# Flamingo block: attention shares split into bf16 parts before they are transposed, and transposed by DMAs

## The reference

```python
x = x + jnp.tanh(g_xattn[0]) * _L0_xattn_ref(_layernorm(x, axis=-1), ctx_512, ...)
x = x + jnp.tanh(g_ffn[0]) * _L0_ffn_ref(_layernorm(x, axis=-1), ...)

# inside _L0_xattn_ref, 16 heads, 128 context rows of 128 channels
q_big = jnp.einsum('bshk,hkq->bshq', q_hk, w_kc_q)
q_r = jnp.einsum('bshq,hqr->bhsr', q_big, W_qr)
k_r = jnp.einsum('bld,hdr->bhlr', kv_rope, W_kr)
scores = jnp.einsum('bhsr,bhlr->bhsl', q_r, k_r)
attn = jax.nn.softmax(scores, axis=-1)
ctx_c = jnp.einsum('bhsl,bld->bhsd', attn, kv_rope)
ctx_lat = jnp.einsum('bhsd,hkd->bshk', ctx_c, w_kc_kv)
out = ctx_lat.reshape(b, s, H * K) @ Wo.T
```

## Time and profile before

| | |
|---|---|
| median of 3 runs | 2187.03 us (2184.39 to 2189.79) |
| span of the profiled execution, first to last instruction | 2184.7 us |
| mean granted TensorE clock over the span | 0.980 |
| PE busy | 2083.8 us, 95% |
| DVE, ACT, POOL busy | 1064.1, 761.5, 621.5 us (49%, 35%, 28%) |
| attention, PE's first to last `o` matmul | 96.2 to about 906 us |
| one step of the attention, mean of a round | 6.48 us |

### The profile page before, as it was taken

The page is one execution under the profiler, slowest core; times in us unless marked ns, Lnnn a source line. Parts: engine busy times, 40 slices in busy tenths (PEclk is TensorE's granted clock), DMA queues, the critical chain, the costliest instruction groups (busy, mean ns, idle before and its releaser), DMA issues.

```text
span 2184.7 us, 35089 instructions
## 1 busy us (share of the span) xinstructions
PE 2083.8 (95%) x13060; PEld 1300.5 (60%) x13060; DVE 1064.1 (49%) x2190; ACT 761.5 (35%) x2089; POOL 621.5 (28%) x680
## 2 busy tenths in 40 slices
PE   7799999999999999895599999999999999999999
PEld 7566666666666666441147777777775444444444
DVE  5776777666666666460134333333332433332333
ACT  4555555555655665320012333333321000000000
POOL 5523333333333452107322223332311220100101
PEclk9999999999999999997699999999999999999999
DMA  8212211111111321321114333333322330211202
GB/s 273 60 38 71 69 61 55 55 55 55 56 62 59 107 78 44 119 70 20 59 40 148 119 113 120 122 116 120 122 89 79 106 140 25 73 50 65 77 15 82
DMA packets 88237, 179.66 MB, mean 82 GB/s; under 512 B 13120, under 2 KB 19008, under 8 KB 88128
## 3 DMA queue, kind: packets, MB, share of 16 engines
q1 hardware_dynamic: 74560, 140.33, 18.9%
q0 software_dynamic: 13568, 37.79, 5.9%
HBM read 121.39 MB, written 56.70 MB: 82 GB/s over the span
## 4 chain that ended last, share of the span: by engine, by line
PE 83%; issue 6%; DVE 6%; ACT 3%; POOL 1%; DMA 1%; DVEq 0%; SPq 0%; ACTq 0%; POOLq 0%
PE score L777 14%; PE o L541 12%; PE score L694 10%; PE o L791 7%; PE p_bank L595 5%; PE m_bank L694 5%; PE p_bank L694 5%; PE o L707 5%; PE c_bank L554 3%; PE score L572 3%; DVE arena L1002 3%; PE c_bank L707 3%; PE t_bank L707 3%; PE t_bank L562 2%; PE p_bank L599 1%
## 5 line engine op out<-in xcount | busy, mean ns | idle before, releaser
L541 PE MATMUL o<-arena 128*128 128x512 bf16 x1536 | 355.0, 380 | 10.6 <-DVE arena L1002 10.6
L777 PE MATMUL score<-arena 128*128 128x256 bf16 (+1 forms) x2880 | 335.1, 272 | 3.2 <-issue 1.7
L777 PEld LDWEIGHTS score<-arena 128*128 128x128 bf16 (+1 forms) x2880 | 292.7, 106 | 44.2 <-issue 2.7
L1362 POOL TENSOR_TENSOR arena<-arena 128x512 f32<-128x512 f32 x128 | 133.2, 1041 | 426.5 <-DVE arena L1018 424.6
L541 PEld LDWEIGHTS o<-arena 128*128 128x128 bf16 x1536 | 148.6, 99 | 171.3 <-DVE arena L1002 16.4
L694 PE MATMUL score<-arena 128*128 128x512 bf16 x1056 | 240.0, 381 | 1.0 <-ACT arena L951 0.7
L829 ACT ACTIVATE arena<-score,arena 128x128 f32<-128x128 f32 x512 | 181.1, 367 | 159.0 <-DVE arena L1042 157.8
L1306 DVE TENSOR_TENSOR arena<-arena,score 128x256 f32<-128x256 f32 (+1 forms) x120 | 50.6, 422 | 307.7 <-ACT arena L971 307.7
L1002 DVE TENSOR_TENSOR arena<-p_bank,arena 64x512 bf16<-64x512 f32 (+1 forms) x184 | 126.9, 690 | 139.9 <-ACT arena L880 119.7
L595 PE MATMUL p_bank<-arena 128*128 128x256 bf16 x1536 | 179.8, 273 | 1.8 <-DVE arena L1002 1.8
L694 PEld LDWEIGHTS score<-arena 128*128 128x128 bf16 x1056 | 102.2, 97 | 132.6 <-issue 5.9
(11 more groups left out here) (157 smaller groups left out, 3126.2 us busy)
## 6 DMA issues: line engine op xcount, KB each, us to landing
xrow_d<-arena SPq DMA_DIRECT2D x80, 256.0 KB, 2.0
arena<-w_expert SPq DMA_DIRECT2D x32, 544.0 KB
...
arena<-x SPq DMA_DIRECT2D x32, 256.0 KB, 4.6
x_d<-arena SPq DMA_DIRECT2D x32, 256.0 KB, 2.0
xn_d<-arena SPq DMA_DIRECT2D x32, 256.0 KB, 4.5
xT_d<-arena SPq DMA_DIRECT2D x32, 256.0 KB, 2.2
```

What stands on the lines that cost most here:

```text
L541: mm = pe.matmul(o_bank[b % 2][:, :], lhsT=cT[:, a, h, :], rhs=M_w[:, w, 4 * hg + h, :], start=(hg == 0 and n == 0), stop=(hg == 3 and n = ...
L777: mm = pe.matmul(gu_bank[n1 % 2][0:IW[j], c * 256:(c + 1) * 256], lhsT=wx[e % 2][:, a, col:col + IW[j]], rhs=xgT[q % 2][:, w, t, :], start ...
L1362: pool.tensor_tensor(prob[:, u % 4], prob[:, u % 4], rden[:, u % 4, :].unsqueeze(2).broadcast_to([P, 4, S]), ALU.mult).then_inc(normed, 1)
```

## The change

The normalised shares are no longer kept as float32 and transposed by PE. POOL's multiplication now writes the high part directly as bf16 in row layout (`share[..., HI]`), and DVE makes the low part from `prob`, `rden` and the high part with four `scalar_tensor_tensor` instructions of 128x128, one for each head (`share_lo`). SP then issues one transposing DMA for each unit, from `share` (128 partitions x 1024 bf16: two parts, four heads) to `pT` (eight 128x128 squares), and PE waits for its landing (`pt_in`) before `c_bank`. PE's transposes, ACT's copy of `pT` high and DVE's `pT` low are gone. `prob` has two buffers in place of four, `share` and `pT` two each; POOL's multiplication of u waits for the landing of unit u-2, ACT's exponentials of u for `share_lo` of u-2. To make room, `zero_ids` now lies on `logits` and ACT waits once for its DMA, and the routing tables move onto a weight ring. Allocations are rounded to 8 words. Inside the loop SP adds a semaphore increment (`turn_begun`) between its wait and the DMA.

The places in the steps: POOL's instruction stays where it was. DVE's four stand where `pT` low stood, between `cT` low and the row maximum, but they are on unit k+3 instead of k+2. SP's DMA stands first in each step.

```diff
@@ -81,11 +81,9 @@
         route_sb = words(2 * P + E)
         token_sb = words(NB).bitcast(I32)
         one, waited = words(1), words(16)
-        zero_ids = words(E * CAP // P).bitcast(I32)
-        logits = words(NB * E).rearrange("p (b e) -> p b e", e=E)
-        slot_of = words(2 * NB).bitcast(I32).rearrange("p (b c) -> p b c", c=2)
-        scatter_to = words(2 * NB).bitcast(I32).rearrange("p (b c) -> p b c", c=2)
-        weight_of = words(2 * NB).rearrange("p (b c) -> p b c", c=2)
+        logits_region = words(NB * E)
+        logits = logits_region.rearrange("p (b e) -> p b e", e=E)
+        zero_ids = logits_region[:, 0:E * CAP // P].bitcast(I32)
 
 
         bm_at = taken[0]
@@ -116,11 +114,13 @@
         rope_a = words(256)
         rope_b = words(256)
 
-        prob_region = words(4 * 512)
-        prob = prob_region.rearrange("p (u h n) -> p u h n", u=4, h=4)
+        prob_region = words(2 * 512)
+        prob = prob_region.rearrange("p (u h n) -> p u h n", u=2, h=4)
+        share = [halves(words(512)).rearrange("p (l h n) -> p l h n", l=2, h=4) for _ in range(2)]
+        pT = [halves(words(512)).rearrange("p (l n) -> p l n", l=2)]
         kr_at = taken[0]
         pT_region = words(512)
-        pT = halves(pT_region).rearrange("p (l n) -> p l n", l=2)
+        pT.append(halves(pT_region).rearrange("p (l n) -> p l n", l=2))
         cT_region = words(512)
         cT = halves(cT_region).rearrange("p (l h n) -> p l h n", l=2, h=4)
         neg_max = words(16).rearrange("p (u h) -> p u h", u=4)
@@ -343,6 +345,13 @@
         def _(sp):
             def step(k, it):
                 m = k % 8
+                u = k + 3
+                if within(u, NU):
+                    wait(sp, share_lo, u + 1, 16, it)
+                    if it is not None:
+                        sp.sem_inc(turn_begun, 1)
+                    sp.dma_start_transpose(pT[u % 2].rearrange("p l (h n) -> p (l h) n", h=4),
+                                           share[u % 2].rearrange("p l h n -> p (l h n)")).then_inc(pt_in[u % 2], 16)
                 if m == 1:
                     g = (k + 23) // 8
                     if within(g, NG):
@@ -546,21 +555,14 @@
                 u = k + 1
                 if within(u, NU):
                     g, b = u // 8, u // 4
-                    wait(pe, pt_lo, u + 1, 16, it)
+                    wait(pe, pt_in[u % 2], 16 * (u // 2 + 1), 128, it)
                     wait(pe, ct_lo, u, 16, it)
                     if u % 8 == 0:
                         wait(pe, ropeN_step, 6 * (g + 1), 12, it)
                     for n, (a, w) in enumerate(PASSES):
-                        mm = pe.matmul(c_bank[:, :], lhsT=kvN[g % 2][:, a, b % 2, :], rhs=pT[:, w, :],
+                        mm = pe.matmul(c_bank[:, :], lhsT=kvN[g % 2][:, a, b % 2, :], rhs=pT[u % 2][:, w, :],
                                        start=(n == 0), stop=(n == 2))
                     mm.then_inc(ct_mm, 1)
-                u = k + 2
-                if within(u, NU):
-                    wait(pe, normed, u + 1, 16, it)
-                    wait(pe, pt_lo, u, 16, it)
-                    for h in range(4):
-                        mm = pe.transpose(t_bank[:, h * S:(h + 1) * S], prob[:, u % 4, h, :], ident_sb)
-                    mm.then_inc(pt_mm, 1)
                 u = k + 4
                 if within(u, NU):
                     g, b, hg = u // 8, u // 4, u % 4
@@ -816,17 +818,14 @@
                 if within(u, NU):
                     wait(act, ct_mm, u + 1, 16, it)
                     act.copy(cT[:, HI].rearrange("p h n -> p (h n)"), c_bank[:, :]).then_inc(ct_hi, 1)
-                u = k + 2
-                if within(u, NU):
-                    wait(act, pt_mm, u + 1, 16, it)
-                    act.copy(pT[:, HI, :], t_bank[:, :]).then_inc(pt_hi, 1)
                 if k % 2 == 1:
                     upper_piece(k + 12, it)
                 u = k + 4
                 if within(u, NU):
                     wait(act, maxed, u + 1, 16, it)
+                    wait(act, share_lo, u - 1, 16, it)
                     for h in range(4):
-                        mm = act.activation(prob[:, u % 4, h, :], score_bank[u % 2][:, h * S:(h + 1) * S], ACT.Exp,
+                        mm = act.activation(prob[:, u % 2, h, :], score_bank[u % 2][:, h * S:(h + 1) * S], ACT.Exp,
                                             bias=neg_max[:, u % 4, h:h + 1], accum_out=den[:, u % 4, h:h + 1])
                     mm.then_inc(exped, 1)
                 if k % 2 == 0:
@@ -937,6 +936,7 @@
                 wait(act, gu_mm, v + 1, 22, it)
                 act.activation(silu[v % 2], gate_bank[v % 2][:, :], ACT.Silu).then_inc(silu_done, 1)
 
+            act.wait_ge(ids_zero, 16)
             run_steps(act, step, NU + 3)
             silu_step(0, None)
             for k in range(NU + 4, LAST_STEP + 1):
@@ -1031,10 +1031,14 @@
                     lower(cT[:, LO].rearrange("p h n -> p (h n)"), c_bank[:, :],
                           cT[:, HI].rearrange("p h n -> p (h n)")).then_inc(ct_lo, 1)
                 links(*((3, 4) if m == 0 else (12, 13)))
-                u = k + 2
+                u = k + 3
                 if within(u, NU):
-                    wait(dve, pt_hi, u + 1, 16, it)
-                    lower(pT[:, LO, :], t_bank[:, :], pT[:, HI, :]).then_inc(pt_lo, 1)
+                    wait(dve, share_hi, u + 1, 16, it)
+                    for h in range(4):
+                        i = dve.scalar_tensor_tensor(out=share[u % 2][:, LO, h, :], in0=prob[:, u % 2, h, :],
+                                                     scalar=rden[:, u % 4, h:h + 1], in1=share[u % 2][:, HI, h, :],
+                                                     op0=ALU.mult, op1=ALU.subtract)
+                    i.then_inc(share_lo, 1)
                 links(*((5,) if m == 0 else (14,)))
                 u = k + 4
                 if within(u, NU):
@@ -1359,9 +1363,10 @@
                 u = k + 3
                 if within(u, NU):
                     wait(pool, inverted, u + 1, 16, it)
-                    pool.tensor_tensor(prob[:, u % 4], prob[:, u % 4],
+                    wait(pool, pt_in[u % 2], 16 * (u // 2), 128, it)
+                    pool.tensor_tensor(share[u % 2][:, HI], prob[:, u % 2],
                                        rden[:, u % 4, :].unsqueeze(2).broadcast_to([P, 4, S]),
-                                       ALU.mult).then_inc(normed, 1)
+                                       ALU.mult).then_inc(share_hi, 1)
                 if m in (4, 5):
                     b = 2 * (c - 1) + m - 4
                     if within(b, NB):
```

12 lines of the change are left out of this document (7 added, 5 removed).

## The result

The changed kernel takes **2368.85 us** (median, 2366.97 to 2371.8) against 2187.47 for the kernel before (2184.39 to 2189.79): a ratio of 1.0833, 95% interval 1.0817 to 1.0848. It is slower by 181 us, where 153 was forecast, and inside the range.

The account below looks back on a forecast made before the run. PE was taken to bound the attention. Waits of 2.3 + 4.9 + 4.1 + 2.0 less 3.5 gave +9.8 us a round, +153 us over 16 rounds after a deduction for the first: 2340 us, range 2235 to 2450.

Parts of the forecast that it names:

- transposes gone: Four PE transposes fewer in each of 128 units: 56 us of PE time, 3.5 us a round gained.
- place 1: Steps 0 and 1: DVE's low shares held up by POOL; PE waits 2.7 before `o` of m = 2, 2.3 more.
- place 2: Load of `x` for m = 3, issued behind the transposing DMA: PE waits 4.9 us before `o` of m = 4.
- place 3: In m = 5 DVE's low shares wait for POOL's multiplication behind its rotary chain: PE waits 4.1 us in m = 6.
- the rest: Smaller waits of the same kind in steps 4 and 7: between 0 and 4, taken as 2.0 us a round.
- What bounds the kernel: The attention is PE bound; an edit that takes work from PE can gain only that, 3.5 us a round.
- The price of the new DVE work: Four new 128x128 DVE instructions: 0.30 each, 0.96 for four against 0.68; 1.4 later in m = 0 beside POOL.
- The clock case: Rival: PE's clock falls to the 1.2 GHz level in the new waits, giving 2404 us; chance 0.15.
- 16 x 4 = 64 more: Low-clock stretches of 2 us at places 2 and 3, in 16 rounds: 64 us on top of the forecast.
- The covers hold better: Rival: only half of the 13.3 of waits appears, +3.1 a round, about 2245 us; chance 0.18.
- The slow transfer: Rival: the transposing DMA takes longer than a step allows, deciding from near 6.5 us; 2640 us or more, chance 0.10.
- Faster: Rival: new waits swallowed if `x` lands in time and POOL's chain ends 4 earlier; 2138 us, chance 0.08.

Follow-up runs that it names:

- dummy matmuls: Changed kernel with 34 unused 512-column matmuls a round added on PE in front of the waits in m = 2, 4 and 6: 2359.07 us.
- PE's part: Kernel before, with three of the four PE transposes of a unit left out from unit 8 on: 2173.65 us, ratio 0.9953.
- the version with all moves: Changed kernel, loads of x first in m = 2, row maximum before low shares, POOL's second rotary chain spread, its first after low shares: 2152.77 us.

## Why the prediction was right, and where it was off

Per round, its terms beside the round of the changed kernel and the round with the dummy matmuls (idle time and dummies together):

| term | forecast | changed kernel | with dummies |
|---|---|---|---|
| transposes gone | -3.5 | -3.5 | -3.5 |
| place 1, less the 0.4 of before | 2.3 | 2.1 | 1.5 |
| place 2 | 4.9 | 4.06 | 4.83 |
| place 3 | 4.1 | 3.26 | 4.23 |
| the rest | 2.0 | none seen | 0.34 + 0.46 + 0.96 = 1.8 |
| PE's work at the low clock | 0 | 54.22 - 47.91 = 6.3 | 4.37 - 2.76 = 1.6 (one group of `o`) |
| sum | 9.8 | 12.2 | 10.4 |
| round, measured, less 51.81 | | 12.20 | 10.83 |

(47.91 is PE's 51.41 of work before, less 3.5. The 6.3 is of the round shown, 5.7 in the mean of the ten; some 0.3 of it are gaps too short to be marked, as PE goes on from the scores in 0.82 and not in 0.65 where it then waits. The 0.4 missing in the last column is mostly of that kind too.)

- **What bounds the kernel, right.** PE's starts were the sums of its own work, so the edit could gain at most 3.5 a round, and the new waits counted in full. (That the 3.5 could all be gained was too high: with DVE as close as it was, under half of PE's part came through when it was taken alone.) The earlier trace rows held the warning: in 500 us only 1.4 of POOL's idle time before its multiplication ended with its own chain, at no cost, and the same order became 4.45 of DVE's time in one round.
- **The price of the new DVE work, close.** 0.346 for one (median) against 0.30, 1.14 for four against 0.96, and 2.08 in m = 0, where the forecast had 412.4 - 410.37 = 2.0. The interpolation between 4 and 512 columns was a little low, and the bound from above, 0.37, was nearer.
- **Place 1, right in size (2.48 against 2.7) and in cause**, shown by the wait in front of POOL's chain.
- **Place 2, right.** Issue 1.23 against 1.0, landing of `x` 6.7 after it against 6.52, wait 4.06 against 4.9; with the clock held up it is 4.83. Shown by the loads put first.
- **Place 3, right as a place**, 3.26 against 4.1 and 4.23 with the clock held up. But its price is not the price of its cure: spread alone, the chain gives nothing, since its last two instructions fall on the next low shares.
- **The rest, right in sum, unseen in the changed kernel.** Waits of 0.46 in m = 7, 0.96 in front of the next m = 0 and 0.34 in m = 4 stand in the round with the clock held up and not in the other.
- **The clock case, wrong in its price.** The forecast itself assumed no low clock, and gave a clock under 0.95 in the attention as a sign against it. The sign came: 0.90. The step that failed is the rival's term "16 x 4 = 64 more": PE's work did slow, by even more (6.3 a round, 100 us), but only some 10 us of it reached the end, in the run that held the clock up. A duration of PE was priced as if PE were the bound, right behind a sentence that made it wait for others.
- **The size.** Of the 29 us between 2340 and 2368.85, some 10 are the clock. The rest lies, as far as the rounds show it, in serial sums that were a little short. By the forecast the four stretches are 14.0, 16.9, 20.0 and 10.7, together 61.6; with the clock held up the first two take 31.8 against 30.9, the third 20.57, the last 10.53. In the round shown, at place 2, each term is short by a bit: the reciprocal ends 6.02 after `o` of m = 2 (5.7 forecast), POOL and the shares take 2.29 (2.12), the issue 1.23 (1.0), the loads 6.73 (6.52). That the waits read 4.06 and 3.26, under the forecast's 4.9 and 4.1, is the other side of the clock: PE arrived late by what its `o` had lost.
- **The covers hold better, false.** That case expected half of the 13.3 of waits. In the mean of the ten rounds PE is idle for 10.2 (0.4 before), and for 14.0 with the dummies counted in.
- **The slow transfer, false.** 3.1 us (3.0 to 4.2) for eight 128x128 blocks, within the forecast's 2 to 5 and near the plain 2.0 to 4.7. PE never waits for it in the regular rounds of this kernel; in the version with all moves it does, for under 1 us at a time. The Trainium skill's "Advanced Engine Details and Errata", section "X-Bar Transpose (TRN2)" (as fast as regular DMAs), agrees with the measurement in size; the 1309 ns a square of "VectorE: DVE Perf Modes", section "The three transpose paths", does not add up over the blocks of one DMA: eight would be 10.5.
- **"Faster", false for this kernel, but near.** The case named two conditions, `x` not late and POOL's chain out of the way; with both, and DVE's order changed, the kernel takes 2152.77 (the case had 2138).
